# Second attention's output projection in split halves, and the heads turned earlier

## The reference

```python
qh = (q @ Wq + bq).reshape(B, LQ, 16, 16).transpose(0, 2, 1, 3)
scores = einsum('bhqd,bhkd->bhqk', qh, kh) * scale
out = einsum('bhqk,bhkd->bhqd', softmax(scores), vh)
concat = out.transpose(0, 2, 1, 3).reshape(B, LQ, 256)
return concat @ Wo + bo
```

## Time and profile before

| | |
|---|---|
| median of 3 runs | 577.41 us (577.17 to 577.84) |
| the profiled execution | 576.48 us, its span 574.8 us |
| granted TensorE clock, mean over the span | 0.955 of full speed |
| busy: PE, DVE, ACT, POOL | 510.5, 424.5, 249.7, 149.9 us |
| L1605, the output projection, 64 matmul records | 18.1 us busy, 379 ns median |
| chain that ended last, by engine | PE 66%, DVE 23%, ACT 2%, POOL 2% |

### The profile page before, as it was taken

How to read it: one execution, slowest core, us unless ns; L and a number is a source line. 1 busy time by engine, 2 the same in 40 slices (tenths; PEclk the granted TensorE clock), 3 DMA queues, 4 the chain that set the end, 5 groups by cost and what they waited for, 6 DMA issues and landing times.

```text
span 574.8 us, 8551 instructions
## 1 busy us (share of the span) xinstructions
PE 510.5 (89%) x3265; PEld 416.4 (72%) x3265; DVE 424.5 (74%) x766; ACT 249.7 (43%) x362; POOL 149.9 (26%) x122
## 2 busy tenths in 40 slices
PE   7888989898979899989999873699999999999990
PEld 3555667797869777777787731389999999999990
DVE  3799779999999985978968859555666848667340
ACT  1233556757585455545565411143444434343200
POOL 2053300000000031202212102810437355283144
PEclk9988989899989999999999985799999999999996
DMA  6511110000000010131221340211446465462031
GB/s 186 172 36 38 37 38 1 1 0 1 1 1 2 0 37 1 39 105 42 74 75 37 129 130 1 82 29 38 105 140 151 116 160 116 137 156 58 5 37 19
DMA packets 35117, 36.39 MB, mean 63 GB/s; under 512 B 3936, under 2 KB 33925, under 8 KB 34949
## 3 DMA queue, kind: packets, MB, share of 16 engines
q1 hardware_dynamic: 28933, 28.19, 15.6%
q0 software_dynamic: 6144, 7.66, 8.0%
HBM read 28.19 MB, written 8.39 MB: 64 GB/s over the span
## 4 chain that ended last, share of the span: by engine, by line
PE 66%; DVE 23%; issue 5%; ACT 2%; POOL 2%; DMA 1%; DVEq 0%; POOLq 0%; ACTq 0%
PE PS L1269 15%; PE PS L1270 14%; PE PS L1271 14%; PE PS L1596 5%; PE PS L1284 4%; PE PS L1477 3%; PE PS L1540 3%; PE PS L1308 2%; DVE st L788 2%; PE PS L1605 2%; DVE xT_lo L812 2%; DVE xn L804 2%; DVE tmp L963 1%; DVE tmp L952 1%; DVE tmp L1152 1%
## 5 line engine op out<-in xcount | busy, mean ns | idle before, releaser
L1269 PE MATMUL PS<-w_hi,hT_hi 128*128 128x256 f32 x384 | 110.6, 288 | 2.5 <-DVE hT_lo L971 1.9
L1270 PE MATMUL PS<-w_lo,hT_hi 128*128 128x256 f32 x384 | 109.6, 286 | 0.0
L1271 PE MATMUL PS<-w_hi,hT_lo 128*128 128x256 f32 x384 | 109.5, 285 | 0.0
L760 ACT ACTIVATE tmp<-PS,biasT 128x512 f32<-128x512 f32 x64 | 40.6, 686 | 109.7 <-PE PS L1271 109.7
L574 POOL DMA_INDIRECT out<-tmp,dst_idx x32 | 55.7, 1742 | 107.6 <-DVE tmp L1228 100.3
L1269 PE MATMUL PS<-xT_hi,w_hi 128*128 128x512 f32 (+1 forms) x200 | 80.5, 403 | 1.1 <-DVE tmp L840 1.1
L1270 PE MATMUL PS<-xT_lo,w_hi 128*128 128x512 f32 (+1 forms) x200 | 78.8, 394 | 0.0
L1271 PE MATMUL PS<-xT_hi,w_lo 128*128 128x512 f32 (+1 forms) x200 | 78.5, 393 | 0.0
L1269 PEld LDWEIGHTS PS<-w_hi,hT_hi 128*128 128x128 f32 x384 | 74.5, 194 | 4.6 <-DVE hT_lo L971 2.3
L1270 PEld LDWEIGHTS PS<-w_lo,hT_hi 128*128 128x128 f32 x384 | 74.5, 194 | 1.2
L1271 PEld LDWEIGHTS PS<-w_hi,hT_lo 128*128 128x128 f32 x384 | 74.6, 194 | 0.0
(11 more groups left out here) (210 smaller groups left out, 964.6 us busy)
## 6 DMA issues: line engine op xcount, KB each, us to landing
w_raw<-in_L_ffn_w SPq DMA_DIRECT2D x72, 256.0 KB, 3.4
residual<-in_x SPq DMA_DIRECT2D x4, 512.0 KB, 6.0
out<-residual SPq DMA_DIRECT2D x3, 512.0 KB, 4.3
normed_rows<-xn SPq DMA_DIRECT2D x3, 512.0 KB, 2.9
kv<-in_L_ffn_b SPq DMA_DIRECT2D x1, 1024.0 KB, 5.8
tmp<-in_L_xattn_Wq SPq DMA_DIRECT2D x2, 256.0 KB
xn<-normed_rows,src_idx POOLq DMA_INDIRECT x32, 3.1
out<-tmp,dst_idx POOLq DMA_INDIRECT x32, 4.0
```

What stands on the lines that cost most here:

```text
L760: act.activation(gD[:, G % 2, f, :], H[:, G % 2, f, :], ACT.Gelu, bias=biasT[:, col:col + 1]).then_inc(e_gelu, 1)
L1269: pe.matmul(o, lh, rh, start=start, stop=False, skip_group_check=skip)
L1270: pe.matmul(o, lh, rl, start=False, stop=False, skip_group_check=skip)
L1271: return pe.matmul(o, ll, rh, start=False, stop=stop, skip_group_check=skip)
```

## The change

The output projection goes over to `split_mm`. ScalarE copies the turned heads of tile t-2 to a rounded high part, concT_hi, where before it copied them plain; VectorE has a new step, `low_heads`, which subtracts this from the bank to make concT_lo, between the iteration's extra work and `normalise`. TensorE waits for the low part (c_ctlo) in place of the copy (c_ctcopied), and makes six products of fp32r in place of two plain ones. The weights wo are split once: the high half by ScalarE at the start of iteration 1, the low half by GpSimd ahead of its index tables. All four halves lie in the hidden buffers hT_hi and hT_lo, numbers 0 and 1, which are not used in this stage; for that ScalarE's wait for the end of the first feed-forward moves to the start of iteration 1. The turn of the heads moves from ahead of product q == 8 to ahead of product q == 4.

```diff
--- before.py
+++ after.py
@@ -174,10 +174,11 @@
         eT = view(2464, 2 * KJ, P)
         qT = view(4096, KD, 512)
         conc = view(6080, 2, D)
-        concT = view(6592, 2, KD, P)
         yC = view(7104, 2, D)
         lgT = view(7616, 512)
         recC = view(8128, 2, HEADS)
+        wo_hi, wo_lo = hT_hi[:, 0, :, 0:D], hT_lo[:, 0, :, 0:D]
+        concT_hi, concT_lo = hT_hi[:, 1, :, 0:D], hT_lo[:, 1, :, 0:D]
         Kblk = kv[:, :].rearrange("p (a b n) -> p a b n", a=2, b=2)
 
 
@@ -313,7 +314,10 @@
         c_pv = sem("c_pv")
         c_conc = sem("c_conc")
         c_ctr = sem("c_ctr")
-        c_ctcopied = sem("c_ctcopied")
+        c_cthi = sem("c_cthi")
+        c_ctlo = sem("c_ctlo")
+        wo_hi_ready = sem("wo_hi_ready")
+        wo_lo_ready = sem("wo_lo_ready")
         c_wo = sem("c_wo")
         c_wofree = sem("c_wofree")
         x3_ready = sem("x3_ready")
@@ -526,6 +530,8 @@
             power(2 * NC)
 
             pool.wait_ge(hT_used, NB_PAIRS)
+            pool.wait_ge(wo_hi_ready, 1)
+            pool.tensor_tensor(wo_lo, wo[:, :, :], wo_hi.bitcast(F32), ALU.subtract).then_inc(wo_lo_ready, 1)
             flag = dict(allow_small_or_imprecise_dtypes=True)
             pool.iota(iota_e, pattern=[[1, NE]], base=0, channel_multiplier=0, **flag).then_inc(rt_consts, 1)
             pool.iota(iota_a, pattern=[[P, 32]], base=0, channel_multiplier=0, **flag).then_inc(rt_consts, 1)
@@ -701,6 +707,10 @@
                 act.activation(lgT[0:NE, 0:n], T[0:NE, 0, 0:n], ACT.Copy).then_inc(lgT_copied, 1)
 
             for t in range(NT + 2):
+                if t == 1:
+                    act.wait_ge(hT_used, NB_PAIRS)
+                    act.wait_ge(late_loaded, 48)
+                    act.activation(wo_hi, wo[:, :, :], ACT.Copy).then_inc(wo_hi_ready, 1)
                 if 1 <= t <= NT:
                     s = t - 1
                     act.wait_ge(c_trA, 2 * s + 1)
@@ -727,15 +737,12 @@
                 if t >= 2:
                     s = t - 2
                     act.wait_ge(c_ctr, s + 1)
-                    act.activation(concT[:, s % 2, :, :], AT1[:, 0:256].rearrange("p (k n) -> p k n", k=2),
-                                   ACT.Copy).then_inc(c_ctcopied, 1)
+                    act.activation(concT_hi[:, s % 2, :], AT1[:, 0:256], ACT.Copy).then_inc(c_cthi, 1)
                 if t < NT:
                     for i, heads in enumerate((slice(0, 12), slice(12, 16))):
                         act.wait_ge(c_shift, 2 * t + 1 + i)
                         act.activation(eC[:, t % 2, heads, :], eC[:, t % 2, heads, :], ACT.Exp, scale=HD ** -0.5
                                        ).then_inc(c_exp, 1)
-                    if t == 1:
-                        act.wait_ge(hT_used, NB_PAIRS)
                     if t % 2 == 1:
                         high_parts(PAIRS + t // 2)
             for d in range(NC - 1, len(PIECES)):
@@ -1048,6 +1055,11 @@
                                   pv[:, :, 0:P].rearrange("p m (h d) -> p m h d", h=HH),
                                   bcast(rc.unsqueeze(3), [P, 2, HH, HD]), ALU.mult).then_inc(c_conc, 1)
 
+            def low_heads(s):
+                dve.wait_ge(c_cthi, s + 1)
+                dve.tensor_tensor(concT_lo[:, s % 2, :], AT1[:, 0:256], concT_hi[:, s % 2, :].bitcast(F32),
+                                  ALU.subtract).then_inc(c_ctlo, 1)
+
             def heads_residual(s):
                 dve.wait_ge(c_wo, s + 1)
                 y = yC[:, s % 2, :]
@@ -1096,6 +1108,8 @@
                         apply(round_of(3, c - 1))
                 if t % 4 == 0 and c >= 2:
                     x_lo(round_of(3, c - 2))
+                if t >= 2:
+                    low_heads(t - 2)
                 if 1 <= t <= NT:
                     normalise(t - 1)
                 if t == NT + 1:
@@ -1587,10 +1601,10 @@
                     for q, jj in enumerate(ORDER):
                         if q == 4:
                             pe.wait_ge(c_copB, s + 1)
+                            if t >= 2:
+                                turn_heads(t - 2)
                         if q == 8:
                             pe.wait_ge(c_copA, 2 * s + 2)
-                            if t >= 2:
-                                turn_heads(t - 2)
                         m, j = divmod(jj, KJ)
                         n = min(P, HK - j * P)
                         ins = pe.matmul(pv[:, m, :], eT[0:n, q, :], Vblk[0:n, j, 2 * b + m, :],
@@ -1600,10 +1614,12 @@
                     turn_heads(t - 2)
                 if t >= 2:
                     s = t - 2
-                    pe.wait_ge(c_ctcopied, s + 1)
+                    pe.wait_ge(c_ctlo, s + 1)
+                    if s == 0:
+                        pe.wait_ge(wo_lo_ready, 1)
                     for k in range(KD):
-                        ins = pe.matmul(AT1[:, 256:512], concT[:, s % 2, k, :], wo[:, k, :],
-                                        start=(k == 0), stop=(k == KD - 1))
+                        heads = [a[:, s % 2, P * k:P * k + P] for a in (concT_hi, concT_lo)]
+                        ins = split_mm(AT1[:, 256:512], heads, (wo_hi[:, k, :], wo_lo[:, k, :]), k == 0, k == KD - 1)
                     ins.then_inc(c_wo, 1)
                 if t % 4 == 1 and c >= 2:
                     logits_rows(c - 2)
```

## The result

The changed kernel takes **585.25 us** (median of 4 runs, 583.84 to 586.81) against 577.29 for the kernel before in the same series: a ratio of 1.0148, 95% interval 1.0117 to 1.0178, so slower by 8.0 us. The range held it (579.0 to 587.8), the sign was right, the forecast of 582.7 was 2.5 us short. The profiled execution took 584.59 us, its span 582.8. Medians and ranges in this document are of all runs; the ratios and their intervals leave out runs over 1.5% above the fastest of the same kernel.

A forecast was written before the change was run, and what follows sets the result against it. TensorE was taken to bound the stage from 198 to 335 us. The terms, 13.7 - 4.0 - 0.64 - 3.7 = +5.3 us, on the median of 577.41 gave 582.7 us, range 579.0 to 587.8.

The forecast's parts named there:

- The low part in VectorE's queue: VectorE's low part stands behind the extra work, so TensorE's projection starts later in late iterations: 13.7 us added.
- the double count that was named: Where VectorE was late by its own work, as in iteration 6, part of the delay was already paid: up to 2 us too much.
- The saving on TensorE: Six split products take 0.72 us where the plain projection took 0.97: 0.25 us saved in each of 16 iterations, 4.0 us.
- the sooner start: With the turn at q == 4, the projection group can start 0.16 us sooner; 0.64 us off over iterations 3, 7, 11 and 13.
- What the delays cover: TensorE's stalls right behind a late projection go: 2.4 us on the bias L1054, 1.3 on exponentials, 3.7 us off.
- The tie: VectorE's residual against GpSimd's weight subtraction, 0.04 us apart in iteration 7; if lost, +9.7 us, 587.1 us, chance 0.25.

The follow-up runs named there:

- the kernel without collisions: The changed kernel, with GpSimd starting each weight subtraction only after VectorE's residual of the same iteration: 579.96 us, ratio 1.0051 to the kernel before.
- the filled waits: The changed kernel with six dummy products on TensorE in each of its five longest waits: 581.27 us, ratio 1.0065 to the kernel before.
- the profile without them: The kernel before, with only GpSimd's wait for VectorE's residual added: 573.66 us, ratio 0.9947.
- the two fastest kernels: The kernel before with GpSimd's wait for VectorE's residual, without and with the turn moved to q == 4: 573.66 and 571.40 us.
- the wait added: The kernel before with the turn moved to q == 4 and GpSimd waiting for VectorE's residual: 571.40 us, ratio 0.9901.

## Why the prediction was right, and where it was short

- **The low part in VectorE's queue.** Right in mechanism, and the term that decides. Expected were 13.7 us, with 12 to 18 us of waits in 10 to 12 iterations; measured 14.4 in 12. Reckoned as in the forecast, as the later start of the projection against the kernel before, it is 13.6 us for 13.7, since 0.72 of iteration 17's 1.42 us were there before. That the sum is so exact is partly luck. The single sizes were less good: iteration 6 waits 2.20 us for the 3.30 of the forecast (the double count that was named), iteration 10 waits 1.87 for 1.06 (1.08 in the kernel without collisions), iteration 17 adds 0.70 for 0.46. Too much and too little cancel.
- **The saving on TensorE.** Six products take 261.61 - 260.81 = 0.80 us, not 0.72, since the second starts 0.21 us after the first, not 0.12. But the group starts 0.26 us sooner instead of 0.16, reckoned from the first weighted value, so the net, 0.43 for 0.41, was right in the four iterations in which VectorE is in time. In the twelve others the sooner start is lost in the wait, and only the shorter group is left, 0.17 us and not 0.25. Over 16 iterations that is 2.7 us for the 4.0 of the sum: this term was 1.3 us too large.
- **What the delays cover.** 2.2 of the 2.4 us on the bias and 1.3 of the 2.7 on the exponentials are gone: 3.5 for 3.7. The kernel that doesn't wait for the low part has more of such stalls (9.4 us), which bears the step out.
- **The tie.** Won by 0.06 us in iteration 7, for a forecast of 0.04, and by 0.05 to 0.07 in 3, 11 and 13. The Trainium skill's rule ("SBUF — State Buffer", "SBUF: two separate sides"), that the first of the two to start keeps the port pair to its end, agrees with these two outcomes: VectorE first by 0.06 us, GpSimd delayed by 0.3; GpSimd first by 0.09 us, VectorE delayed by 2.1. It does not agree with the recorded starts of iteration 13 of the filled waits (VectorE first by 0.05 us, and delayed by 2.2). Whether the order there or only its record is other than the rule says stays open; a tie this close could have gone the other way, and that all four were won was luck as much as forecast. But only iterations built like 7 had been looked at. Iteration 9, where before the residual came first by 0.55 us, wasn't, and there VectorE lost: the early turn lets GpSimd start sooner, and the wait on the low part makes the residual late. With the early turn alone VectorE lost there too (GpSimd first at 278.29 us, against 278.57).
- **The term that was missing** is the clock. The prediction took the granted 1.00 of the earlier trace rows as fixed. Of the profile's +8.6 us in the stage, 3.0 are the half clock of iteration 11 and 5.6 the mechanism, for 5.3 forecast. That these two agree is again in part a balance of misses: the terms as measured give 13.6 - 2.7 - 1.0 - 3.5 = 6.4 us, and some 0.7 of it is won back in the last iteration, whose bias starts 1.56 us behind its projection and not 2.25. The remaining difference to the +8.1 of the two profiled executions is 1.1 us lost ahead of the stage, and 1.6 won behind it.
- **The price of the collisions** of the kernel before, which the prediction left in place, is 1.1 us in the stage by the profile without them. That of one more, in iteration 9, was larger, since the next iteration's wait is 1.87 us with it and 1.08 without, and the fall of the clock came behind that.

Open: what share of the 5 us of the run without collisions is clock. In its profile the stage is 3.1 us shorter than the change's, as much as the stretch costs, but a single profile doesn't prove a share of a median. That the falls follow from TensorE's standing still is made likely by several things: the filled waits; the two fastest kernels, which have no fall between 200 and 335 us; and the place of the falls, each of which, in every profile here, begins less than 3 us behind the end of a stand of TensorE of 1.00 to 3.03 us, whatever it waited for. It is not the whole cause: in the change the stands of 1.85, 2.06 and 2.20 us in iterations 2, 5 and 6 have no fall behind them, and neither has the one of 1.33 us in the kernel before.

## What to carry to other kernels

A step that is cheap and has ample idle time on its engine costs by its place in the queue: read when the engine reaches that place, and not how busy it is. Before work is moved earlier, see what else on the other engines moves with it; here a free gain of 0.16 us per iteration turned into a loss of 5 us because two unrelated operations then started in the other order, 0.09 us apart, and one semaphore wait turned it into a gain. Where operations of VectorE and GpSimd are ordered by luck alone, order them by hand before anything near them is tuned.

## What the runs showed of the hardware

- A margin of 0.05 to 0.09 us between two recorded starts goes with 2.1 us more or less of one VectorE operation. It came out alike in all seven odd iterations of the early turn and in both profiles of the change, but at 0.05 us it went both ways (iteration 13, the change and the filled waits).
- TensorE's granted clock fell to half for stretches of 3.4 to 10.2 us, most of them 6.8, within a stage in which it was 89% busy (129.78 of 146 us), at a cost of 3.0 us for 6.8 where TensorE is the bound (12.02 us in the change for 8.98 without the collisions; 11.91 with the early turn for 8.86 with the wait added). Each began behind a stand of TensorE of 1.00 to 3.03 us, but as long stands were often followed by none. The same program had it at the same iteration in two profiles; small edits moved it, doubled it or took it away. Several kernels' runs spread by 6 to 11 us (dummy products: 577.0 to 587.2), but the four of the best lie within 0.24 us (571.36 to 571.60).
